# Split weight rows moved to a pitch of 4864 bytes

## The chip, the cores and the metric

The kernel runs on one core of one Trainium2 chip. The metric is the device time of one execution in microseconds; of several runs the median is taken. The kernel before took 495.64 us, the median of three runs (495.01 to 495.94).

## What is computed

For 64 batches x[b] is 64 channels by 1024. Each batch has a condition that picks one of 16 matrices of 64 x 64. In the reference's terms, cut to what matters:

```
y      = einsum('bct,bcd->bdt', x, cond_weights[condition])       # 64 x 64 per batch
logits = y @ gate_w.T                                              # 8 experts
w_full = softmax of the two largest logits, at their experts, 0 elsewhere
result = y @ base_w.T + base_b
low    = y @ lora_A[e].T        for the 8 experts, rank 16         # 128 columns in all
result = result + 2 * sum_e w_full[e] * (low[e] @ lora_B[e].T)
out    = x + result
```

All is float32. The products keep float32 accuracy by splitting each operand into a high part (rounded to the type fp32r) and a low part (what is left), and adding three products: high by high, high by low, low by high.

## The kernel before

**Tiling.** Two batches form a pair, 128 rows of y. There are 32 pairs, and one step of the kernel works on each (0 to 31). The big product of a step is y of the pair, 128 x 1024, times a joint weight matrix of 1024 x 1160: 1024 output columns, 128 columns of lora_A and 8 of the gate. Its contraction runs over 8 blocks of 128 rows (KT = 8, index k). The 1160 columns are cut into three PSUM banks (BANKS, line 58): columns 0 to 384, 384 to 768 and 768 to 1160.

**Buffers.** `w_hi` and `w_lo` (lines 77 and 78) hold the split weights, `[128, 8, 1160]` each: in a partition, row k has 1160 elements, 4640 bytes, and the rows follow each other directly. `y_hi` and `y_lo` hold the split y of two pairs, `[128, 2, 8, 128]`: block k of a pair is 512 bytes in a partition. All SBUF tensors are allocated by `sb` (line 69), in the order of lines 76 to 121: `w_raw`, `w_hi`, `w_lo`, then `lb_raw` and the others, `y_hi` and `y_lo` late.

**Order of TensorE.** For each k, the step (line 711) runs the three products of PRODUCTS (line 637), y_hi with w_hi, y_hi with w_lo, y_lo with w_hi, and for each the three banks. `project` (line 639) is one matmul: a 128 x 128 block of y is loaded as the stationary operand, and 384 or 392 columns of a weight row move past it. So a step has 8 x 9 = 72 of these matmuls. The same block of y is loaded anew for each of the three banks. Between them stand `mix` of later pairs (line 662, two matmuls of 512 columns, before k = 0 and after k = 1) and, after k = 6, the nine `experts` matmuls of the pair before (line 674), which add low times lora_B.

Step 0 (`first_step`, line 678) runs, for each k, the two products with w_hi, and those with w_lo one k later. The last step (`last_step`, line 742) takes one bank at a time, 2, 0, 1, and in each runs k and then the three products, so every matmul there loads another block than the one before it.

**Around it.** ScalarE rounds y to its high part (line 386), moves pieces for the transpose (line 363) and copies out of PSUM (line 355). VectorE transposes (474), makes the low parts (459, 481, 535), adds the accumulators to the result (548, 551) and works out the gates (489 to 522). GpSimd adds the bias and picks the condition's weights. Loads and stores go through SyncE's queue. The order on each engine is written out by hand and semaphores tie them. At the start ScalarE (`w_high`, line 336) and VectorE (`w_low`, line 446, and line 568) fill `w_hi` and `w_lo` from `w_raw`, one row k at a time; afterwards only TensorE reads them.

Of the kernel before, what the change touches and what calls it, by code (L numbers as in the profile page):

```python
# [8 lines left out]
F32R = mybir.dt.float32r  # L9
# [4 lines left out]
P = 128  # L14
# [4 lines left out]
def adaln_ffn_kernel(  # L19
# [24 lines left out]
    N = proj_w.shape[1]  # L44
    NE = N - O - ER
    RANK = ER // NE
    KT = T // P
# [6 lines left out]
    assert 2 * CH == P and ER == P and T == 2 * 512 and PAIRS % 4 == 0 and O == T  # L54


    BW = 384
    BANKS = [(0, BW), (BW, 2 * BW), (2 * BW, N)]
    TAIL = O - 2 * BW
    RANKS = (TAIL, TAIL + ER)  # L60
    GATES = (TAIL + ER, TAIL + ER + NE)
    assert GATES[1] <= 512 and BW + P <= 512

# [4 lines left out]
    with ExitStack() as ctx:  # L68
        def sb(name, shape, dt):
            return ctx.enter_context(nc.sbuf_tensor(name, shape, dt))  # L70
# [3 lines left out]


        w_raw = sb("w_raw", [P, KT, N], F32)
        w_hi = sb("w_hi", [P, KT, N], F32R)
        w_lo = sb("w_lo", [P, KT, N], F32R)
        lb_raw = sb("lb_raw", [P, O], F32)
        lb_hi = sb("lb_hi", [P, O], F32R)  # L80
        lb_lo = sb("lb_lo", [P, O], F32R)
# [111 lines left out]
        def lowT_block(c):  # L193

            return acc[:, c % 2, 0, BW:BW + P]

# [14 lines left out]
        def _(sp):  # L211
# [48 lines left out]
            sp.wait_ge(res_ready, PAIRS)  # L260
            sp.dma_start(out_pairs[LAST, :, 0:BW], res[:, LAST % 4, 0:BW]).then_inc(stored[LAST % 4], 16)
            sp.dma_start(out_pairs[LAST, :, 2 * BW:O], res[:, LAST % 4, 2 * BW:O]).then_inc(stored[LAST % 4], 16)
            sp.wait_ge(res_ready, PAIRS + 1)
# [552 lines left out]
```

## Time and profile before

| | |
|---|---|
| median of the runs | 495.64 us |
| the profiled execution | 495.63 us |
| its span, first to last instruction | 493.5 us |
| TensorE busy | 488.4 us, 99% of the span |
| ScalarE, VectorE, GpSimd busy | 77%, 75%, 26% |
| DMA, mean rate over the span | 89 GB/s |
| granted TensorE clock | 1.000 of full |

Busy time of a matmul in the profile overlaps the next one's: each record of 384 columns lasts about 0.34 us, while the next begins some 0.17 us after it. What a matmul costs is therefore read from the distance of the starts, in the timeline or in the chain of work.

### The profile page before, as it was taken

To read this page: it belongs to the slowest core of one execution; us is meant where nothing else is said; L and a number is where in the kernel's file an instruction comes from. 1 tells how busy PE (TensorE), PEld (TensorE's weight loads), DVE (VectorE), ACT (ScalarE), POOL (GpSimd) and SP (SyncE) were. 2 spreads that over 40 slices of the span, in tenths; PEclk is the share of its full clock that TensorE was granted. 3 is DMA by queue.
4 is the path that set the end of the run, shared out by engine and by line. 5 is a ranking of instruction groups with operands and counts; after the bars stand their busy time and mean duration, and the time that the engine had idled before them with its cause. 6 is when DMAs were issued, how large, how long until landed. Compare 5 with 4: busy or idle time off the path is not lost.

```text
span 493.5 us, 8737 instructions
## 1 busy us (share of the span) xinstructions
PE 488.4 (99%) x2771; PEld 480.8 (97%) x2771; DVE 370.8 (75%) x800; ACT 382.4 (77%) x740; POOL 129.8 (26%) x111
## 2 busy tenths in 40 slices
PE   8999999999999999999999999999999999999997
PEld 8998999999999999999999999999999999999997
DVE  4988877778787778787787777787877787777653
ACT  4898778878778887788787788887788877887620
POOL 2033202333113333033332223332133320233120
PEclk9999999999999999999999999999999999999999
DMA  8812122121221221221222222212212212211112
GB/s 335 349 42 88 60 90 94 56 93 59 92 90 61 88 96 52 92 90 53 96 66 79 89 79 69 96 53 90 90 53 96 92 54 88 96 53 54 56 42 85
DMA packets 31986, 43.89 MB, mean 89 GB/s; under 512 B 18402, under 2 KB 22498, under 8 KB 31970
## 3 DMA queue, kind: packets, MB, share of 16 engines
q1 hardware_dynamic: 31826, 43.17, 25.2%
q10 hardware_dynamic: 144, 0.52, 0.3%
q8 instruction: 8, 0.13, 0.1%
q14 instruction: 8, 0.07, 0.0%
HBM read 25.00 MB, written 18.68 MB: 89 GB/s over the span
## 4 chain that ended last, share of the span: by engine, by line
PE 91%; DMA 3%; ACT 3%; DVE 1%; SPq 1%; issue 1%; ACTq 0%
PE acc L642 76%; PE acc L674 9%; PE mixed L662 5%; DMA x_sb<-in_x 3%; ACT y_moved L363 1%; SPq L219 1%; ACT x_parts L350 1%; DVE w_raw L467 0%; ACT w_raw L355 0%; DVE w_raw L548 0%; DVE w_raw L551 0%; SPq L215 0%; DVE y_turned L474 0%; DVE y_lo L481 0%; ACT y_hi L386 0%
## 5 line engine op out<-in xcount | busy, mean ns | idle before, releaser
L363 ACT COPY y_moved<-w_raw 32x256 f32<-32x256 f32 x480 | 194.3, 405 | 38.0 <-DVE w_raw L467 32.3
L642 PE MATMUL acc<-w_hi,y_hi 128*128 128x384 f32 (+1 forms) x768 | 180.0, 339 | 0.6 <-DVE w_raw L548 0.4
L642 PE MATMUL acc<-w_hi,y_lo 128*128 128x384 f32 (+1 forms) x768 | 179.4, 338 | 0.0
L642 PE MATMUL acc<-w_lo,y_hi 128*128 128x384 f32 (+1 forms) x768 | 179.0, 338 | 0.0
L295 POOL TENSOR_TENSOR w_raw<-x_sb,bias 128x1024 f32<-128x1024 f32 x32 | 77.3, 2416 | 345.7 <-DVE low L522 277.8
L642 PEld LDWEIGHTS acc<-w_hi,y_hi 128*128 128x128 f32 x768 | 137.4, 188 | 6.9 <-DVE w_raw L548 0.8
L642 PEld LDWEIGHTS acc<-w_hi,y_lo 128*128 128x128 f32 x768 | 138.7, 188 | 0.0
L642 PEld LDWEIGHTS acc<-w_lo,y_hi 128*128 128x128 f32 x768 | 138.6, 188 | 0.0
L467 DVE TENSOR_TENSOR w_raw<-mixed,w_raw 64x1024 f32<-64x1024 f32 x60 | 73.0, 1217 | 30.5 <-ACT w_raw L355 30.1
L474 DVE STREAM_TRANSPOSE y_turned<-y_moved 128x512 f32<-128x512 f32 x60 | 42.2, 705 | 51.8 <-ACT y_moved L363 51.8
L355 ACT COPY w_raw<-mixed 64x1024 f32<-64x1024 f32 x60 | 60.8, 1014 | 21.9 <-PE mixed L662 20.6
L459 DVE TENSOR_TENSOR x_parts<-x_sb,x_parts 64x1024 fp32r<-64x1024 f32 x60 | 74.0, 1233 | 2.6 <-ACT x_parts L350 0.8
L350 ACT CAST x_parts<-x_sb 64x1024 fp32r<-64x1024 f32 x60 | 62.8, 1047 | 2.4 <-DMA x_sb<-in_x 1.6
L386 ACT CAST y_hi<-y_turned 128x512 fp32r<-128x512 f32 x60 | 37.3, 622 | 20.6 <-DVE y_turned L474 20.6
L286 POOL CAST w_sel<-cw_parts 128x128 fp32r x60 | 52.1, 895 | 3.9 <-PE mixed L648 3.6
L481 DVE TENSOR_TENSOR y_lo<-y_turned,y_hi 128x512 fp32r<-128x512 f32 x60 | 41.5, 692 | 3.1
L662 PE MATMUL mixed<-x_parts,w_sel 128*128 128x512 f32 x120 | 37.7, 395 | 0.2 <-DVE w_raw L467 0.2
L548 DVE TENSOR_TENSOR w_raw<-acc,w_raw 128x768 f32<-128x768 f32 x31 | 29.6, 955 | 1.9 <-PE acc L674 1.9
L674 PE MATMUL acc<-lb_hi,lowT_hi 128*128 128x384 f32 (+1 forms) x96 | 30.6, 319 | 0.0
L674 PE MATMUL acc<-lb_hi,lowT_lo 128*128 128x384 f32 (+1 forms) x96 | 30.6, 318 | 0.0
L674 PE MATMUL acc<-lb_lo,lowT_hi 128*128 128x384 f32 (+1 forms) x96 | 30.5, 318 | 0.0
L662 PEld LDWEIGHTS mixed<-x_parts,w_sel 128*128 128x128 f32 x120 | 21.8, 187 | 0.7 <-issue 0.7
(52 smaller groups left out, 237.9 us busy)
## 6 DMA issues: line engine op xcount, KB each, us to landing
x_sb<-in_x SPq DMA_DIRECT2D x32, 512.0 KB, 3.3
out<-w_raw SPq DMA_DIRECT2D x31, 512.0 KB, 2.6
w_raw<-in_proj_w SPq DMA_DIRECT2D x8, 580.0 KB, 9.5
scratch<-low_squares SPq DMA_DIRECT2D x29, 64.0 KB, 1.5
lowT_raw<-scratch SPq DMA_DIRECT2D x116, 16.0 KB, 1.8
cw<-in_cond_w ACTq DMA_DIRECT2D x1, 512.0 KB, 3.5
lb_raw<-in_lora_b SPq DMA_DIRECT2D x1, 512.0 KB, 16.4
bias<-in_base_b SPq DMA_DIRECT2D x1, 512.0 KB, 17.1
```

The source lines that it names most:

```text
L286: nc.gpsimd.tensor_copy(w_sel[:, c % 2, b, :].rearrange("p (h d) -> p h d", d=CH), cw_parts[:, :, bass.ds(cond * CH, CH)]).then_inc(sel_re ...
L295: nc.gpsimd.tensor_tensor(res[:, c % 4, :], x_sb[:, c % 4, :], bias[:, :], ALU.add) \
L350: nc.scalar.copy(x_parts[half, c % 2, b, :], x_sb[half, c % 4, :]).then_inc(x_hi_ready, 1)
L355: nc.scalar.copy(y_rest[:, b, :], mixed[CH:P, :, :]).then_inc(rest_ready, 1)
L363: done = nc.scalar.copy(y_moved[q * SQ:(q + 1) * SQ, g, :, :], piece.rearrange("m (k q a) -> m q k a", q=QUARTERS, a=SQ)[:, q, :, :])
L459: nc.vector.tensor_tensor(x_parts[there, c % 2, b, :], x_sb[here, c % 4, :], x_parts[here, c % 2, b, :].bitcast(F32), ALU.subtract).then_i ...
L467: nc.vector.tensor_tensor(y_sum[:, b, :].rearrange("m (h t) -> m h t", h=2), mixed[0:CH, :, :], y_rest[:, b, :].rearrange("m (h t) -> m h ...
L474: nc.vector.transpose(y_turned[:, :, ks, :], y_moved[:, :, ks, :]).then_inc(turned, 1)
L481: nc.vector.tensor_tensor(low_part, turned_half(h), high, ALU.subtract).then_inc(y_ready, 1)
L642: return nc.tensor.matmul(acc[:, c % 2, b, 0:hi - lo], y_part[:, c % 2, k, :], w_part[:, k, lo:hi], start=(k == 0 and product == 0), stop= ...
L662: last = nc.tensor.matmul(mixed[:, h, :], w_sel[:, c % 2, b, :], x_parts[:, c % 2, b, h * 512:(h + 1) * 512], start=True, stop=True)
L674: last = nc.tensor.matmul(acc[:, c % 2, b, 0:hi - lo], low_part[:, :], lb_part[:, lo:hi], start=False, stop=(low_part is lowT_lo), skip_gr ...
```

## The change

The two weight tensors get rows of 1216 elements (4864 bytes) and the kernel uses 1160 of each, from element 48 (192 bytes) on. `w_hi` and `w_lo` become views into them with the same shape as before, so that no other line changes. The two tensors are together 3584 bytes a partition longer, and all that is allocated behind them stands that much higher.

```diff
+    PITCH, FIRST = 1216, 48
     BW = 384
     BANKS = [(0, BW), (BW, 2 * BW), (2 * BW, N)]
     TAIL = O - 2 * BW
...
         w_raw = sb("w_raw", [P, KT, N], F32)
-        w_hi = sb("w_hi", [P, KT, N], F32R)
-        w_lo = sb("w_lo", [P, KT, N], F32R)
+        w_hi_rows = sb("w_hi_rows", [P, KT, PITCH], F32R)
+        w_lo_rows = sb("w_lo_rows", [P, KT, PITCH], F32R)
+        w_hi = w_hi_rows[:, :, FIRST:FIRST + N]
+        w_lo = w_lo_rows[:, :, FIRST:FIRST + N]
         lb_raw = sb("lb_raw", [P, O], F32)
```

## Rows read from the trace of the kernel before

**Rows 1.** Page, busy us (share of the span) and instructions of TensorE.

```profile
PE 488.4 (99%) x2771; PEld 480.8 (97%) x2771; DVE 370.8 (75%) x800; ACT 382.4 (77%) x740; POOL 129.8 (26%) x111
```

**Rows 2.** Page, chain that ended last, shares by engine.

```profile
PE 91%; DMA 3%; ACT 3%; DVE 1%; SPq 1%; issue 1%; ACTq 0%
```

**Rows 3.** Waits of TensorE: us in total, times, longest.

```profile
PE acc L642 <- DVE w_raw L548: 0.4, 1, 0.4
...
PE mixed L662 <- DVE w_raw L467: 0.2, 1, 0.2
```

**Rows 4.** Chain of work, one steady step: start us, us, what, how many.

```profile
399.64 0.47 PE mixed L662 x2
400.11 3.16 PE acc L642 x18
...
403.73 7.93 PE acc L642 x45
411.66 1.40 PE acc L674 x9
413.06 1.59 PE acc L642 x9
```

**Rows 5.** Timeline of TensorE, two steady steps: start us, us, line, operation, count.

```profile
223.41 0.69 PE L642 MATMUL acc<-w_hi,y_hi 128*128 128x384 f32 x3
...
228.18 0.69 PE L642 MATMUL acc<-w_hi,y_hi 128*128 128x384 f32 x3
...
229.78 0.69 PE L642 MATMUL acc<-w_hi,y_hi 128*128 128x384 f32 x3
230.30 0.68 PE L642 MATMUL acc<-w_lo,y_hi 128*128 128x384 f32 x3
230.82 0.69 PE L642 MATMUL acc<-w_hi,y_lo 128*128 128x384 f32 x3
231.34 0.34 PE L674 MATMUL acc<-lb_hi,lowT_hi 128*128 128x384 f32 x1
...
234.80 0.69 PE L642 MATMUL acc<-w_hi,y_hi 128*128 128x384 f32 x3
...
244.79 0.69 PE L642 MATMUL acc<-w_hi,y_hi 128*128 128x384 f32 x3
...
246.35 0.34 PE L674 MATMUL acc<-lb_hi,lowT_hi 128*128 128x384 f32 x1
```

**Rows 6.** Timeline of VectorE, the same step.

```profile
230.71 0.25 DVE L535 TENSOR_TENSOR lowT_lo<-lowT_raw,lowT_hi 128x128 fp32r<-128x128 f32 x1
...
231.53 1.49 DVE L481 TENSOR_TENSOR y_lo<-y_turned,y_hi 128x512 fp32r<-128x512 f32 x2
```

**Rows 7.** Timeline of TensorE, step 0, k = 5 and k = 6.

```profile
17.34 0.69 PE L642 MATMUL acc<-w_hi,y_hi 128*128 128x384 f32 x3
...
18.40 0.69 PE L642 MATMUL acc<-w_lo,y_hi 128*128 128x384 f32 x3
18.93 0.69 PE L642 MATMUL acc<-w_hi,y_hi 128*128 128x384 f32 x3
...
19.98 0.69 PE L642 MATMUL acc<-w_lo,y_hi 128*128 128x384 f32 x3
```

**Rows 8.** Timeline of TensorE, last step: bank 0 at k = 0, 6, 7; bank 1 begins.

```profile
480.40 0.34 PE L642 MATMUL acc<-w_hi,y_hi 128*128 128x384 f32 x1
...
483.55 0.34 PE L642 MATMUL acc<-w_hi,y_hi 128*128 128x384 f32 x1
...
484.08 0.34 PE L642 MATMUL acc<-w_hi,y_hi 128*128 128x384 f32 x1
...
484.61 0.34 PE L642 MATMUL acc<-w_hi,y_hi 128*128 128x384 f32 x1
```

**Rows 9.** Groups of instructions that fill the split weights and a like one: busy, mean ns.

```profile
L459 DVE TENSOR_TENSOR x_parts<-x_sb,x_parts 64x1024 fp32r<-64x1024 f32 x60 | 74.0, 1233 | 2.6 <-ACT x_parts L350 0.8
...
L446 DVE TENSOR_TENSOR w_lo<-w_raw,w_hi 128x1160 fp32r<-128x1160 f32 x8 | 10.7, 1360 | 0.9 <-ACT w_hi L336 0.7
...
L336 ACT CAST w_hi<-w_raw 128x1160 fp32r<-128x1160 f32 x7 | 8.2, 1167 | 2.4 <-DMA w_raw<-in_proj_w 2.3
```

## The prediction, made before the changed kernel ran

> **What bounds the kernel.** I read the page's busy times first: TensorE is busy 99% of the span [rows 1]. Busy alone proves little, so next comes the chain that ended last: 91% of it is TensorE [rows 2], and TensorE's own waits are a few tenths of a microsecond, each met once in the whole run [rows 3]. So what a matmul takes from its start to the next one's start goes into the time one to one. The chain cut by pieces then gives a steady step: 0.47 for one pair of mixes, 3.16 for k = 0 and 1, the other mixes, 7.93 for k = 2 to 6, 1.40 for the nine expert matmuls, 1.59 for k = 7 [rows 4]. The piece of 7.93 us stands 29 times in the chain with the same length; these are steps 2 to 30. The period is 244.79 - 229.78 = 15.01 us [rows 5]. The weight matmuls hold 3.16 + 7.93 + 1.59 = 12.68 us of it, for 72 of them, 176 ns each.
>
> **What differs between the blocks k.** All 72 do the same work, so a difference by k must come from addresses, from history or from what runs beside them. Bytes first, from the declarations: each tensor between `w_hi` and `y_lo` is a multiple of 256 bytes long in a partition (37120 for a weight tensor), so if they stand one behind the other, which I assume, all begin at the same residue modulo 256. Blocks of y are 512 bytes and keep that residue. Weight rows are 4640 = 18 x 256 + 32 bytes, so row k stands 32k bytes off the blocks of y: 0, 32, 64, ... 192 for k = 6, 224 for k = 7. The banks start 1536 = 6 x 256 bytes apart and change nothing in that.
>
> Now the starts. k = 6 begins at 229.78 and the experts behind it at 231.34, 1.56 us; one period later 244.79 and 246.35, 1.56 again [rows 5]. Each product of it, three matmuls, takes 0.52. The other blocks: k = 5 from 228.18 to 229.78, 1.60; k = 2 to 5 from 223.41, 6.37 in all, 1.592 each; k = 7 1.59; k = 0 and 1 1.58 each. Block 6 is the shortest, and with rounding of the starts I put it at 1.565. It has the offset that the change gives to all eight.
>
> **The change, part by part.**
>
> (1) No instruction is added, removed or moved on any queue; every access keeps its element count and its run of 1160 (or 384, 392) elements without a gap. What remains is addresses.
>
> (2) Steady steps. The new pitch is 19 x 256 bytes, and 48 elements are 192, so each row k is 192 off the blocks of y. The two tensors grow by 14 x 256 bytes together, so nothing else changes its residue: the expert matmuls and the mixes (all at the same residues as before) keep 1.40 and 0.93. If each k then takes what k = 6 takes: 8 x 1.565 = 12.52, against 12.68, 0.16 us less. Thirty steps (1 to 30; step 1 has the same matmuls with the mixes elsewhere): 4.8 us. Bounds: the fastest product seen is 0.52, and 24 of these are 12.48, 0.20 less, 6.0 us in thirty steps; the slowest block seen is 1.60, and 8 of these are 12.80, 0.12 more, 3.6 us in all. I take 4.8 because the rows of k = 6 are the only ones at this offset, and both its products with `w_hi` and the one with `w_lo` show 0.52, though these two tensors differ by 256 bytes modulo 512. That speaks for 256 bytes being the length that counts: the change does alter multiples of 256, which so far were the same for all k.
>
> (3) Step 0. There k = 5 with its two products takes 18.40 - 17.34 = 1.06 and k = 6 19.98 - 18.93 = 1.05 [rows 7]. So the difference is smaller there, 0.01 in six matmuls; I take 0.1 us for the step, between 0 and 0.16.
>
> (4) Last step. Bank 0 from its first matmul up to the first matmul of bank 1 is 484.61 - 480.40 = 4.21, 0.526 a block of three matmuls, and k = 6 is 484.08 - 483.55 = 0.53 [rows 8]. Nothing is gained there: I take 0, between -0.1 and +0.1.
>
> (5) Filling the weights. The eight subtractions take 1.360 us for 1160 elements, 1.17 ns an element, and a like one with other addresses and lanes 1.233 for 1024, 1.20 ns [rows 9]. That 0.03 ns is the most I can find by which addresses might matter: 8 x 1160 x 0.03 = 0.3 us either way, for which I take 0. The copies of `w_hi` are the same case.
>
> (6) What comes next once TensorE is faster. The second subtraction for the next y ends at 231.53 + 1.49 = 233.02 and the step that needs it begins at 234.80 [rows 5, 6]: 1.8 us to spare. The tightest is lowT, ready at 230.71 + 0.25 = 230.96 and needed at 231.34: 0.38 us. The blocks k = 0 to 6 ahead of it would shrink by 0.14 at most by (2), so 0.24 is left. No new wait.
>
> Sum: 4.8 + 0.1 + 0 = 4.9 us. The profiled execution took 495.63 us, 2.1 more than its span of 493.5, and that part has no matmul in it. It lies on the median of 495.64, so 495.6 - 4.9 = 490.7 us, 1.0% less.
>
> The Trainium skill speaks against all this. Its page "TensorE: Matmul & The Clock Gate" (section "Back-to-back issue gap") has a matmul of N columns follow the last after N / 2.4 + 2.5 ns, 162.5 ns for 384 columns, whatever the addresses. "SBUF — State Buffer" (section on SBUF's two separate sides) adds that TensorE has its own ports and never waits on anyone. By these rules block 6 has no reason to be faster and the time stays 495.6. The trace disagrees with the first: 176 ns a matmul, and 0.52 against 0.53 for three of the same shape by their k. The second it neither shows nor refutes: TensorE's two reads, stationary and moving, may still meet each other.
>
> **The rivals.**
>
> *The offset isn't what makes block 6 short* (no change, 495.6 us). The place in the step could: ScalarE's long run of moves ends just as k = 6 begins, and VectorE changes over to transposes. For it: steps 0 and 31, with other neighbours, show little or nothing of the effect [rows 7, 8]. Against it: the piece of 7.93 us is the same in 29 steps, in the ones where DMAs fall differently too, and k = 7, 0 and 1, where those moves are not running, are at 1.58 to 1.59 and not at 1.56. To this rival I count the case that the tensors don't stand as I assume, so that the distances aren't 192 at all.
>
> *Part of it* (about 493.3 us). The gain depends on what came before, such as the step from another offset into block 6, and with all rows alike the matmuls settle between 1.57 and 1.58: 0.16 halved, 30 x 0.08 = 2.4 us.
>
> *The other side: slower* (499.2 us). Until now row k and block k of y were the same multiple of 256 apart for all k, but for the 32k. With 4864 against 512 bytes the distance grows by 4352 = 17 x 256 from row to row, so multiples of 256 that never occurred come up. If two reads of TensorE meet by an address pattern longer than 256 bytes, the rows may all come out like k = 5, 1.60: 0.12 us a step more, 3.6 us. It decides as soon as the mean block passes 12.68 / 8 = 1.585 us. For it: the last step, where block 6 in another order is no shorter than its neighbours [rows 8]. Against it: the equal 0.52 of `w_hi` and `w_lo` in block 6.
>
> **How the numbers follow.** Forecast 0.62, part of it 0.10, no change 0.14, slower 0.14. A change under 0.2%, 1 us, counts as none, about what a measurement of this kernel can tell. Faster is then 0.72, same 0.14, slower 0.14. The range: from 489.4 (6.0 from the fastest product, with 0.2 of step 0 and the last) to 495.9, which takes in the partial gain and no change, and leaves out the slower case and a little below, not quite 2 in 10. The likeliest case's own range is 489.4 to 491.7.
>
> **What would show it.** In the profile after, the number of instructions and each group's mean should stand as before, the expert piece at 1.40 and the mixes at 0.46 to 0.47. The pieces of the chain should be 3.13 for k = 0 and 1, 7.83 for k = 2 to 6 and 1.57 for k = 7, the period 14.85. If k = 3 to 5 lie at 1.60 still and k = 6 at 1.565, the offset was not the cause. If some k are short and others long, in a pattern that repeats, multiples of 256 count. A new wait of TensorE on VectorE's L535 would show that (6) was wrong. I am wrong altogether if the period is 15.0 or more.

## The result, and the profile after

The changed kernel took 497.07 us (median of eight runs, 496.49 to 497.44), the kernel before 495.56 in eight (495.01 to 495.94): a ratio of 1.0031 with an interval of 1.0022 to 1.0040. It is slower by 1.5 us, 0.3%. Forecast were 490.7 us and, with a chance of 0.14, 499.2. The profiled execution of the changed kernel took 496.49 us, 0.86 more than the one before; it is the lowest of the eight, so some 0.6 us of the difference of medians isn't in this profile.

All lines of the kernel are four lower in the file: 642 is now 646, 662 is 666, 674 is 678.

The page of the kernel after, busy times and chain by engine, against [rows 1, 2]:

```profile
PE 489.6 (99%) x2771; PEld 482.7 (98%) x2771; DVE 372.1 (75%) x800; ACT 382.3 (77%) x740; POOL 129.9 (26%) x111
...
PE 94%; ACT 3%; DVE 1%; DMA 1%; issue 0%; SPq 0%; ACTq 0%
```

The same number of instructions, and TensorE still sets the end. One steady step in its chain of work (start us, us, what, how many), against [rows 4]:

```profile
400.22 0.46 PE mixed L666 x2
400.68 3.20 PE acc L646 x18
403.88 0.45 PE mixed L666 x2
404.33 8.00 PE acc L646 x45
412.33 1.40 PE acc L678 x9
413.73 1.56 PE acc L646 x9
```

k = 0 and 1 went from 3.16 to 3.20, k = 2 to 6 from 7.93 to 8.00, k = 7 from 1.59 down to 1.56, both pairs of mixes from 0.93 to 0.91, the experts stayed. The step is 15.07 us long, before 15.01.

The timeline of TensorE shows where within a step it turns, against [rows 5]:

```profile
228.09 0.69 PE L646 MATMUL acc<-w_hi_rows,y_hi 128*128 128x384 f32 x3
...
229.69 0.69 PE L646 MATMUL acc<-w_hi_rows,y_hi 128*128 128x384 f32 x3
...
231.28 0.34 PE L678 MATMUL acc<-lb_hi,lowT_hi 128*128 128x384 f32 x1
...
232.69 0.69 PE L646 MATMUL acc<-w_hi_rows,y_hi 128*128 128x384 f32 x3
233.21 0.68 PE L646 MATMUL acc<-w_lo_rows,y_hi 128*128 128x384 f32 x3
233.73 0.68 PE L646 MATMUL acc<-w_hi_rows,y_lo 128*128 128x384 f32 x3
234.25 0.62 PE L666 MATMUL mixed<-x_parts,w_sel 128*128 128x512 f32 x2
```

k = 5 takes 229.69 - 228.09 = 1.60, k = 6 1.59, and behind the experts k = 7 takes three times 0.52. With the starts read to the nanosecond, blocks 0 to 5 are alike: the three banks take 177, 176 and 181 ns, 533 or 534 together, and the same for the next product, 1.600 us a block (the expectations below round it up to 1.602). I call this the long rhythm. Block 7 has 173, 173, 177 and then twice 173, 170, 177, which is 520 for three: the short rhythm, 1.563 us for this block and 1.560 for one that has it throughout. Same instructions, same distance modulo 256, two rhythms. Block 6, which had 1.566 before, now has 1.598, and block 7 is the short one. So the place in the step had not made block 6 short.

Step 0, where no mix of 512 columns has run yet, k = 5 and 6, against [rows 7]:

```profile
17.23 0.68 PE L646 MATMUL acc<-w_hi_rows,y_hi 128*128 128x384 f32 x3
...
18.27 0.68 PE L646 MATMUL acc<-w_lo_rows,y_hi 128*128 128x384 f32 x3
18.79 0.68 PE L646 MATMUL acc<-w_hi_rows,y_hi 128*128 128x384 f32 x3
...
19.82 0.68 PE L646 MATMUL acc<-w_lo_rows,y_hi 128*128 128x384 f32 x3
```

18.27 - 17.23 = 1.04 and 19.82 - 18.79 = 1.03, before 1.06 and 1.05: the short rhythm, with the very rows that take 1.60 in steady steps. A mix of 512 columns behind it doesn't always end it: in step 2 of this profile blocks 2 to 5 take 1.560 to 1.563 behind the second pair of mixes, which lasted 0.54 us there and not 0.45. The last step, bank 0, behind the experts, against [rows 8]:

```profile
481.31 0.34 PE L646 MATMUL acc<-w_hi_rows,y_hi 128*128 128x384 f32 x1
...
484.43 0.34 PE L646 MATMUL acc<-w_hi_rows,y_hi 128*128 128x384 f32 x1
...
484.95 0.34 PE L646 MATMUL acc<-w_hi_rows,y_hi 128*128 128x384 f32 x1
...
485.47 0.34 PE L646 MATMUL acc<-w_hi_rows,y_hi 128*128 128x384 f32 x1
```

4.16 us for eight blocks of three, 0.52 each, before 4.21.

The balance of the two profiled executions, from the starts of the matmuls: 27 steady steps (3 to 29) cost 0.060 us more each, 1.62; step 30 0.07 more; steps 0 to 2 45.89 us instead of 46.68, 0.79 less, of which 0.19 is step 0 and 0.32 a shorter wait in the first pair of mixes of step 2 (0.66 us instead of 0.98); the last step 0.05 less. That is 0.85 of the 0.86.

### The profile page after: what moved, and what is told of

It is laid out like the page before. It is cut to its first block, busy times and chain, and to the rows that moved or that the text cites. A ratio compares the mean times of both kernels' runs of the same rounds, so it can differ in the third digit from the quotient of the medians.

```text
span 494.4 us, 8737 instructions
## 1 busy us (share of the span) xinstructions
PE 489.6 (99%) x2771; PEld 482.7 (98%) x2771; DVE 372.1 (75%) x800; ACT 382.3 (77%) x740; POOL 129.9 (26%) x111
## 4 chain that ended last, share of the span: by engine, by line
PE 94%; ACT 3%; DVE 1%; DMA 1%; issue 0%; SPq 0%; ACTq 0%
PE acc L646 79%; PE acc L678 9%; PE mixed L666 5%; ACT y_moved L367 2%; DMA x_sb<-in_x 1%; PE mixed L652 1%; ACT w_raw L359 0%; DVE y_turned L478 0%; DVE w_raw L471 0%; DVE w_raw L552 0%; DVE w_raw L555 0%; DVE y_lo L485 0%; ACT y_hi L390 0%; ACT y_hi L344 0%; ACT w_hi_rows L340 0%
## 5 line engine op out<-in xcount | busy, mean ns | idle before, releaser
L646 PE MATMUL acc<-w_hi_rows,y_hi 128*128 128x384 f32 (+1 forms) x768 | 180.5, 339 | 0.3 <-ACT w_hi_rows L340 0.3
L646 PE MATMUL acc<-w_lo_rows,y_hi 128*128 128x384 f32 (+1 forms) x768 | 179.7, 339 | 0.0
L646 PE MATMUL acc<-w_hi_rows,y_lo 128*128 128x384 f32 (+1 forms) x768 | 179.7, 338 | 0.0
L646 PEld LDWEIGHTS acc<-w_hi_rows,y_hi 128*128 128x128 f32 x768 | 137.6, 188 | 6.1 <-DVE w_raw L552 0.5
L646 PEld LDWEIGHTS acc<-w_hi_rows,y_lo 128*128 128x128 f32 x768 | 139.1, 188 | 0.0
L646 PEld LDWEIGHTS acc<-w_lo_rows,y_hi 128*128 128x128 f32 x768 | 139.0, 188 | 0.0
L471 DVE TENSOR_TENSOR w_raw<-mixed,w_raw 64x1024 f32<-64x1024 f32 x60 | 73.0, 1216 | 31.1 <-ACT w_raw L359 30.7
```

The costliest lines, as they stand in the source:

```text
L471: nc.vector.tensor_tensor(y_sum[:, b, :].rearrange("m (h t) -> m h t", h=2), mixed[0:CH, :, :], y_rest[:, b, :].rearrange("m (h t) -> m h ...
L646: return nc.tensor.matmul(acc[:, c % 2, b, 0:hi - lo], y_part[:, c % 2, k, :], w_part[:, k, lo:hi], start=(k == 0 and product == 0), stop= ...
```

## The experiments

The theory from here on: with all rows at one distance the weight matmuls settle into a rhythm, there is more than one at the same distance, and the matmuls before decide which. The rivals are that a row's addresses alone set its time (multiples of 256 bytes included), and that the other engines at that place do.

**Shorter mixes.** The changed kernel with

```diff
-                for h in range(2):
-                    last = nc.tensor.matmul(mixed[:, h, :], w_sel[:, c % 2, b, :],
-                                            x_parts[:, c % 2, b, h * 512:(h + 1) * 512], start=True, stop=True)
+                for q in range(4):
+                    h, part = q // 2, slice(q % 2 * 256, (q % 2 + 1) * 256)
+                    last = nc.tensor.matmul(mixed[:, h, part], w_sel[:, c % 2, b, :],
+                                            x_parts[:, c % 2, b, q * 256:(q + 1) * 256], start=True, stop=True)
```

> The changed kernel, with each mix cut into four matmuls of 256 columns instead of two of 512. Theory (rhythm): with all weight rows at the same distance, the weight matmuls fall into one of two repeating rhythms, 177, 176, 181 ns (534 for three, a block of 1.602 us) or 173, 170, 177 (520, 1.560), and the matmuls just before decide which; after a mix of 512 columns it is the long one, after the expert matmuls, which end on 256 columns, the short one. If the last length matters, blocks k = 0 to 6 fall to 1.56, the weight matmuls of a step from 12.77 to 12.5 and the time from 497.1 to about 489 to 491 (the two more matmuls of each mix cost 5 to 10 ns each, 0.4 us in all). If the rhythm is set by the mix's addresses and not its length, the time stays within 1 us of 497.5. Rival (addresses of the row alone, multiples of 256 included): no weight matmul changes. Rival (neighbours): what the other engines do at k = 7 and in step 0 makes those fast; no weight matmul changes here either.

Measured: 491.8 us in one run. Its chain of work, one step:

```profile
411.41 0.47 PE mixed L667 x4
411.88 3.13 PE acc L646 x18
415.01 0.47 PE mixed L667 x4
415.48 7.81 PE acc L646 x45
```

In 25 of the 27 steps 3 to 29 the blocks are at 1.56 but for some 10 ns behind each mix and one wait; in the other two, steps 3 and 13, k = 1 to 6 take mostly 1.58, a third rhythm that comes up again below. No weight matmul, no address and no other engine's work was touched, and 0.26 us went out of the weight matmuls of a step (12.76 to 12.50, by its pieces). Both rivals fall. The edit changes two things of a mix, the length of its matmuls and their number, and no run parts the two. In five runs:

> The changed kernel with both mixes in matmuls of 256 columns, timed: 491.5 to 492, ratio 0.992 to 0.993. It differs from the changed kernel in nothing but the length of the mixes' matmuls, so it carries the claim that the mixes set the rhythm.

Measured: 491.16 us (490.80 to 492.03), ratio 0.9921 (0.9908 to 0.9935). This is the fastest of the versions with several runs, 4 us below the kernel before. The same edit on the old rows was not run, so how much of the 4 us needs the new rows isn't shown.

**A mix in another place.** The changed kernel, its first mix before the experts:

```diff
-                if ahead and c >= 2:
-                    mix(j, c + 1, 0)
...
+                        if ahead_next:
+                            mix(j, c + 2, 0)
                         pe.wait_ge(lowT_ready, s)
                         for b in range(3):
                             last = experts(c - 1, b)
```

> The changed kernel, with the first half of the next mix moved from before k = 0 to before the expert matmuls of the step before (after k = 6), all work the same. Theory (rhythm): no mix stands between the experts and k = 2 now but the one after k = 1; so k = 7, 0 and 1 keep the short rhythm (1.56) and only k = 2 to 6 have the long one (1.602). That is 0.084 us a step less than the changed kernel, 14.99, or 2.5 us in 30 steps: 494.6. Rivals: addresses of the row alone, or the neighbours at k = 7: k = 0 and 1 stay 1.60 and the time 497.

Measured: 490.5 us in one run, 4 us less than I had expected of my own theory: k = 7, 0 and 1 are short as forecast, but k = 2 to 6 too, behind a mix of 512 columns, in all but three steps.

> The changed kernel with the mix moved, once more and timed. From the one look: blocks of 1.56, 490.5 us. Expected 490 to 491.5, a ratio of 0.990 to 0.992 to the kernel before.

Measured: 491.82 us (491.69 to 491.99), ratio 0.9929 (0.9912 to 0.9945), a little above what I expected. In this profile 8 of the 27 steps 3 to 29 have k = 2 to 6 in the long rhythm. Two of them side by side in its chain:

```profile
399.86 8.00 PE acc L646 x45
...
414.88 7.81 PE acc L646 x45
```

By the starts block 3 takes 1600 or 1601 ns in these eight steps and 1559 to 1561 in all others, nothing between. What differs is some ns ahead of them: the last matmul before the mix takes 179 to 187 in the eight, in the others mostly 175 to 178, though 185 occurs too. So a mix doesn't always start the long rhythm, and small shifts in time go with it; whether they tip it, and by which rule, isn't shown.

**The same move with the old rows.**

> The kernel before (rows of 4640 bytes) with only the mix moved to before the expert matmuls. Theory (rhythm): with rows at eight distances there is no short rhythm to keep, so the weight matmuls stay at 12.6 to 12.7 a step and the time at 494.5 to 496. Rival (moving the mix is the gain by itself, by a wait or by a shorter step): 490.5 to 492, as with the new rows.

Measured: 495.47 us (495.05 to 495.75), ratio 1.0000 (0.9990 to 1.0009). The chain has the old length for k = 2 to 6:

```profile
403.02 7.93 PE acc L643 x45
```

Moving the mix is worth nothing by itself, the new rows cost 1.5 us by themselves, and the two together save 3.7.

**An extra matmul behind the mixes.** The changed kernel with, ahead of the products:

```diff
+                    if k in (0, 2) and 2 <= c < PAIRS - 2:
+                        nc.tensor.matmul(acc[:, c % 2, 0, BW:BW + P], y_hi[:, c % 2, k, :], w_hi[:, k, 0:P],
+                                         start=False, stop=True, skip_group_check=True)
```

> The changed kernel with one matmul more after each pair of mixes: 128 columns of the block's own operands, written to 128 unused columns of the accumulator's first bank (the result of it is never read), before k = 0 and before k = 2 in steps 2 to 29. Theory (rhythm, with memory): the mix of 512 columns doesn't put the weight matmuls into the long rhythm, it lets it pass on, and anything that disturbs the sequence can end it. If the extra matmul ends it, blocks k = 0 to 6 fall from 1.602 to 1.56, 0.29 us a step, and it costs two times 0.06: 497.1 - 8.5 + 3.4 = about 492. If it passes the rhythm on or there is no such memory (rival: addresses alone, or the neighbours), it only costs: 500.5.

Measured: 495.58 us (495.23 to 496.00), ratio 1.0003 (0.9994 to 1.0013). In the chain (L726 is the extra matmul):

```profile
403.58 0.46 PE mixed L666 x2
404.04 0.06 PE acc L726
404.10 7.85 PE acc L646 x45
```

The rhythm is ended: 7.85 us instead of 8.00, and by the starts every block is 173, 170, 177 but for the first matmul. That one takes 225 ns. The extra matmul costs 60 + 52 = 0.112 us and not 0.06, so that 2 x 0.112 eats most of what is won. That an extra matmul ends the rhythm was right, its price was wrong. Whether a mix only lets the long rhythm pass on, as the expectation has it, this run can't tell; the next one can.

**Only one of them.** The same with k == 0 in place of k in (0, 2):

> The changed kernel with the one extra matmul of 128 columns only before k = 0 (steps 2 to 29), none after the second mix. Theory (a mix of 512 columns starts the long rhythm, the rhythm then lasts until something ends it): k = 0 and 1 come down to 1.56, the mix after k = 1 starts the long rhythm again, k = 2 to 6 stay at 1.602. The step: 15.073 - 0.084 + 0.112 (what the extra matmul cost in the run with two) = 15.10, the time about 498. Rival (only the mix before k = 0 starts it and the second one passes on what it finds): k = 2 to 6 at 1.56 too, 14.89, about 491.5.

Measured: 497.73 us in one run, the step 15.107 us:

```profile
205.48 3.17 PE acc L646 x18
...
209.11 8.00 PE acc L646 x45
```

As the theory has it, and to 0.3 us of the forecast: k = 0 and 1 at 1.56 (3.17 holds the 0.05 of the first matmul), and the mix after k = 1 starts the long rhythm afresh. Here the mix after k = 1 does it in every step from 3 to 29. So the idea of the run before, that a mix only passes the long rhythm on, was wrong.

**The start of 192 bytes alone.** Rows still 32 bytes more than a multiple of 256 apart:

```diff
-    PITCH, FIRST = 1216, 48
+    PITCH, FIRST = 1224, 48
```

> The start of 192 bytes alone: FIRST = 48 kept, but rows of 1224 elements, 4896 bytes, which is 32 more than a multiple of 256 as before the change. So the rows are 192 + 32k off the blocks of y (192, 224, 0, 32, ...), all different. Theory (rhythm): no rhythm can repeat over blocks; each block has its own transient, and the sum over all eight residues is about that of the kernel before: a step of 15.0, 495 to 496. k = 0, at 192, comes behind a mix. Rival (the residue of a row fixes its time): k = 0 is 1.565, k = 2 1.58, k = 5 to 7 1.597, the same sum. It differs from the theory in whether each residue keeps its time in another place.

Measured: 496.66 us (496.11 to 497.03), ratio 1.0022 (1.0012 to 1.0032). The timeline, first product of k = 0, 1, 2 to 6, and the experts:

```profile
401.11 0.70 PE L646 MATMUL acc<-w_hi_rows,y_hi 128*128 128x384 f32 x3
...
402.70 0.69 PE L646 MATMUL acc<-w_hi_rows,y_hi 128*128 128x384 f32 x3
...
404.75 0.69 PE L646 MATMUL acc<-w_hi_rows,y_hi 128*128 128x384 f32 x3
...
406.33 0.69 PE L646 MATMUL acc<-w_hi_rows,y_hi 128*128 128x384 f32 x3
...
407.91 0.69 PE L646 MATMUL acc<-w_hi_rows,y_hi 128*128 128x384 f32 x3
...
409.49 0.69 PE L646 MATMUL acc<-w_hi_rows,y_hi 128*128 128x384 f32 x3
...
411.09 0.69 PE L646 MATMUL acc<-w_hi_rows,y_hi 128*128 128x384 f32 x3
...
412.69 0.34 PE L678 MATMUL acc<-lb_hi,lowT_hi 128*128 128x384 f32 x1
```

By residue modulo 256, in ns of a block, the mean of steps 3 to 29:

| off the blocks of y | 0 | 32 | 64 | 96 | 128 | 160 | 192 | 224 |
|---|---|---|---|---|---|---|---|---|
| before (k = 0 to 7) | 1581 | 1583 | 1576 | 1597 | 1598 | 1596 | 1566 | 1587 |
| start alone (k = 2 to 7, 0, 1) | 1581 | 1583 | 1577 | 1600 | 1599 | 1600 | 1583 | 1588 |

Here the rival was right for seven of eight: a residue keeps its time, to 4 ns, in another place of the step and at other multiples of 256; 32 repeats its nine intervals (176 175 178, 171 175 175, 174 180 178) to a nanosecond. Only 192 doesn't keep it. Behind a mix, at k = 0, it takes 1583, with 526 in the last product, the third rhythm again. So the length that counts is 256 bytes, as I had assumed, and of the eight 192 is the one at which the time is seen to hang on what went before. The median of 496.66 lies above the 495 to 496 of the expectation. One thing no run parts: the blocks of y never moved modulo 256, so what counts may be how far a weight row is from them, or where the row itself stands.

**Other distances for all rows.** FIRST = 0, 16 and 52 in the changed kernel:

> The changed kernel with FIRST = 0: each row 0 instead of 192 modulo 256 off the blocks of y. Theory (rhythm): again a pattern of three that repeats in every block, with one or two levels depending on what went before. Block 0 of the kernel before, at this distance, had 174, 174, 178 twice in a row after a mix, 526 for three: 1.578 a block, 12.62 a step, 14.93 the step with mixes of 0.93, so about 493. Rival (addresses alone with multiples of 256): blocks differ from each other or are 1.60, above 496.

> The changed kernel with FIRST = 16: each row 64 modulo 256 off the blocks of y. Theory (rhythm): one pattern for all blocks after a mix; block 2 of the kernel before, which came after a mix, had 173 177 179, 172 176 177, 169 176 177 (1.576, the last two products 1.568 at that pace): 12.6 a step, about 492 to 493.5. Rival (addresses with multiples of 256): 496 or more.

> The changed kernel with FIRST = 52: each row 208 modulo 256 off the blocks of y. If it is the residue modulo 256 in steps of 32 bytes that matters, this behaves like 192 (15.07) or like 224 (k = 7 of the kernel before, 177 173 177 and 177 175 177 for three, 1.58 to 1.587 a block, a step of 15.0). If finer steps matter, something else. In all cases one or two patterns that repeat.

Measured, one run each: 494.46, 493.15 and 498.75 us. The piece of k = 2 to 6 in the chain of each:

```profile
402.70 7.90 PE acc L646 x45
```

```profile
401.59 7.88 PE acc L646 x45
```

```profile
406.32 8.00 PE acc L646 x45
```

At 0 every block settles on 174 174 178, forecast from the old block 0, and the step is 14.99 us where I had put 14.93: the block behind the experts takes 1.588, the others 1.580 to 1.583 where I had put 1.578. At 64 the nine intervals change from block to block, 1.568 to 1.581 a block, in line with the old 1.576; the one pattern for all blocks that I expected isn't there, so rows at one distance don't always settle on one. At 208 it is 177 174 182, 533 for three, in blocks 0 to 6, as long as the long rhythm of 192 (177 176 181) but spread otherwise, and block 7 takes 1.598, where it had 1.563 at 192. So finer steps than 32 bytes matter. These single runs rank distances; differences under 1 us between them are not shown.

**Both edits.** The first mix moved and only the second one cut:

> The changed kernel with the first mix moved to before the experts, and the second one, after k = 1, cut into four matmuls of 256 columns. In the run with only the first edit some steps took 15.00 instead of 14.83, because the second mix let the long rhythm in. Theory: behind 256 columns it doesn't start, all steps are 14.83 to 14.84, the time 490.3 to 490.9 with less spread. Rival (the long rhythm comes in by chance, from whatever wait or mix): some steps stay at 15.00, 491.5 or more.

Measured: 493.44 us (492.93 to 494.10), ratio 0.9960 (0.9947 to 0.9974). The theory of the last length failed: nearly all steps are 14.93 to 14.95 us, with

```profile
207.73 7.91 PE acc L646 x45
```

for k = 2 to 6, by the starts 175 177 174, 526 or 527 for three: the third rhythm, the one that ends k = 0 in the run with the start alone. Of the steps 3 to 29 two took 14.83 us and one 15.02. Behind matmuls of 256 columns the long rhythm is rare, but they don't choose the short one by themselves. It is one more rhythm at the same distance, and I have no rule that tells which comes. The rival in the expectation was nearer, with a rhythm it didn't know.

## Why the prediction was wrong

The step that failed is (2), "if each k then takes what k = 6 takes". The row was read rightly and was the only one at 192. But it was one context: a block that came behind k = 5 at another distance, never behind a mix and never behind its own kind. The prediction priced a block by its addresses, as if it had no memory. At 192 the same nine matmuls take 1.560, 1.58 or 1.600 us, and seven of eight blocks of a steady step got the slowest. In the terms of the sum: -0.16 us a step was forecast for the weight matmuls, and they gave +0.08 (12.68 to 12.76); the mixes, which I had unchanged, gave -0.02. Together that is the +0.060 of a step.

The evidence for it stood in my own rows. In the last step block 6 took 0.53 like the others [rows 8], at the same distance in another order. I wrote this into the slower rival and into "part of it", and then gave the two 0.24 together. A distance that is short in one order of matmuls and not in another has a time that depends on order, and the change gave no reason to expect block 6's order everywhere. That part of the rival was right, and so was the size of a block, 1.60. Its time, 499.2, was too high: block 7 was short, the mixes were, and the steps 0 to 2 and the last took 0.84 us less. Its mechanism, multiples of 256 that never occurred, was wrong: the start-alone run has new multiples too and keeps seven residues' times. The equal 0.52 of `w_hi` and `w_lo` had pointed there.

(1), the unchanged instructions, held. (3), step 0, was too small: 0.19 against 0.1 and a bound of 0.16, for nearly all its matmuls got the short rhythm. (4), the last step, gained 0.05, inside its bounds. (5) and (6) held: no wait of note appeared in a step. The assumed layout is only borne out in part: rows a multiple of 256 bytes apart behave alike at 192, 0 and nearly so at 208, and the start-alone run moves the residues as the declarations say. That all tensors begin at the same residue, so that a distance called 192 is 192, no run shows.

The rival "the offset isn't what makes block 6 short" is refuted: blocks 6 and 7 swapped roles after the change. One thing said against it was wrong: k = 1 runs from 221.36 to 222.95, and three of ScalarE's moves (L363) begin at 222.33, so they do run there. The Trainium skill, "TensorE: Matmul & The Clock Gate" (section "Back-to-back issue gap"), gives N / 2.4 + 2.5 ns, 162.5 for 384 columns. The prediction took this for the rule of a stream; the section gives it for a matmul by itself and says that it comes out too high for long matmuls in a stream with weight loads. Neither fits here: in this stream the smallest mean, the short rhythm, is 520 / 3 = 173 ns, and the long one 178. The measurements decide. The Trainium skill, "SBUF — State Buffer" (section on SBUF's two separate sides), has TensorE never wait on anyone. No run here shows a wait on a port or refutes one; what they show is that with nothing but the start of the weight rows moved, from 64 to 208 bytes, the kernel went from 493.15 to 498.75 us, one run each.

What stays open: what in the chip carries the rhythm, why a mix of 512 columns mostly starts the long one, and which rhythm follows a given sequence. That cutting or moving the mixes changes it is shown. That the two reads of TensorE meet in SBUF is a guess that no run tests; moving the blocks of y by some bytes under unmoved weight rows would be a first test.

## What to carry to other kernels

Where TensorE is full, read the distance of the starts of its matmuls by block and by what ran before them, not only their mean; a difference of 2 to 3% hides there. Before one fast block is copied to all, look for the same addresses in another order of work; if these are not fast, the block's time is not its own. If rows are aligned all alike, the rhythm that follows is decided by the matmuls in between, so change both together and measure: here the rows alone cost 0.3%, with shorter mixes they save 0.8%. What the shorter mixes save on the old rows wasn't measured; for the moved mix it was, and it is nothing.

## What the hardware showed that I had not expected

- The same stream of fp32r matmuls, same addresses modulo 256, runs at 173, 175.5 or 178 ns a matmul (520, 526 or 533 for three), each for dozens of matmuls on end, at a granted clock of 1.0.
- One matmul of 128 columns behind a mix costs 112 ns: 60 of its own and 52 at the next one, which takes 225 instead of 173.
- Distances that differ by 16 bytes (192 and 208) have different patterns; those that differ by a multiple of 256 have the same block time to 4 ns, at the seven that could be compared.
- Two profiled executions of one kernel, on two chips, had 3 and 8 long steps of 27, and took 490.50 and 491.69 us. At 0.18 us a step the five account for 0.9 of the 1.2.
